# The causal mask of the diagonal scores: a second, accumulating bf16 matmul in place of a select on GpSimd

## What is computed

```python
q = (x @ wq_w.T + wq_b).reshape(b, t, H, HD)        # b=2, t=2048, H=32, HD=32
k1, v1 = x @ wk_w.T + wk_b, x @ wv_w.T + wv_b       # one head for keys and values
scores = jnp.einsum('bqhd,bkd->bhqk', q, k1) / jnp.sqrt(jnp.float32(HD))
scores = jnp.where(causal, scores, -jnp.inf)
weights = jax.nn.softmax(scores, axis=-1)
attn = jnp.einsum('bhqk,bkd->bqhd', weights, v1).reshape(b, t, H * HD)
x = _layernorm(x + attn @ wo_w.T + wo_b)
x = _layernorm(x + ffn(x))      # ffn: scaled, clipped x times scaled, clipped weight, scaled back
```

## Time and profile before

| | us |
|---|---|
| three runs, median (lowest to highest) | 2768.05 (2760.64 to 2773.67) |
| profiled execution: span | 2772.0 |
| the run nearest to that span | 2773.67 |
| PE busy | 2549.6 (92%) |
| DVE busy | 1861.1 (67%) |
| ACT busy | 1276.1 (46%) |
| POOL busy | 843.5 (30%) |

### The profile page before, as it was taken

How to read it: one execution, slowest core, us unless ns; L and a number is a source line. 1 busy time by engine, 2 the same in 40 slices (tenths; PEclk the granted TensorE clock), 3 DMA queues, 4 the chain that set the end, 5 groups by cost and what they waited for, 6 DMA issues and landing times.

```text
span 2772.0 us, 45699 instructions
## 1 busy us (share of the span) xinstructions
PE 2549.6 (92%) x15400; PEld 1588.9 (57%) x15400; DVE 1861.1 (67%) x1428; ACT 1276.1 (46%) x1571; POOL 843.5 (30%) x568
## 2 busy tenths in 40 slices
PE   6999994989999999999888999999999998699998
PEld 5888883544555444444455554554444446588887
DVE  6333335557688898989646677898898894444444
ACT  2222222545566766677425556666676671100000
POOL 2321302423222221231323323232212314466663
PEclk9999996889999999999889999999999998799999
DMA  6343334522111120110224112111101013122221
GB/s 231 119 151 129 121 121 128 133 51 65 50 39 39 39 57 20 38 38 27 66 83 121 51 38 66 39 50 38 39 27 38 12 28 144 46 91 91 91 91 61
DMA packets 78806, 201.42 MB, mean 73 GB/s; under 512 B 8704, under 2 KB 10752, under 8 KB 76544
## 3 DMA queue, kind: packets, MB, share of 16 engines
q1 hardware_dynamic: 51936, 142.11, 18.0%
q10 hardware_dynamic: 26784, 58.21, 5.5%
HBM read 125.83 MB, written 74.45 MB: 72 GB/s over the span
## 4 chain that ended last, share of the span: by engine, by line
PE 77%; issue 6%; DVE 4%; POOL 4%; ACT 4%; DMA 2%; ACTq 1%; SPq 1%; DVEq 0%; POOLq 0%
PE bank L1112 16%; PE bank L1153 15%; PE bank L1100 14%; PE bank L1044 13%; PE bank L1201 13%; ACT prob L678 4%; POOL prob L537 3%; PE bank L1129 3%; PE bank L1121 2%; DMA q_st<-max_d 1%; DVE acc L907 1%; PE bank L1190 1%; PE bank L1028 1%; DMA xt_raw<-x_t 0%; DVE acc L904 0%
## 5 line engine op out<-in xcount | busy, mean ns | idle before, releaser
L678 ACT ACTIVATE prob<-bank 128x1024 f32<-128x1024 f32 (+3 forms) x1280 | 1075.7, 896 | 656.1 <-PE bank L1112 611.7
L907 DVE TENSOR_TENSOR acc<-acc,prob 128x2048 f32<-128x2048 f32 (+3 forms) x512 | 1073.8, 2097 | 171.6 <-POOL prob L537 131.0
L1112 PE MATMUL bank<-q_st,k_st 98*128 98x512 f32 (+3 forms) x2560 | 700.3, 391 | 62.6 <-DMA q_st<-max_d 31.7
L1153 PE MATMUL bank<-prob,v_sb 128*32 128x512 f32 (+3 forms) x5120 | 614.8, 553 | 67.2 <-POOL prob L537 65.0
L1112 PEld LDWEIGHTS bank<-q_st,k_st 98*128 98x128 f32 x2560 | 430.0, 193 | 376.1 <-ACT prob L678 266.3
L537 POOL TENSOR_SCALAR_AFFINE_SELECT prob<-prob 128x512 f32<-128x512 f32 x256 | 282.5, 1106 | 929.4 <-ACT prob L678 928.5
L1153 PEld LDWEIGHTS bank<-prob,v_sb 128*32 128x32 f32 x5120 | 101.8, 109 | 267.9 <-issue 159.3
L1044 PE MATMUL bank<-xt_hi,w_hi 128*128 128x512 f32 x576 | 226.5, 393 | 14.8 <-DVE xt_lo L765 14.8
L1044 PE MATMUL bank<-xt_hi,w_lo 128*128 128x512 f32 x576 | 226.1, 393 | 0.0
L1044 PE MATMUL bank<-xt_lo,w_hi 128*128 128x512 f32 x576 | 225.7, 392 | 0.0
L1201 PE MATMUL bank<-wf_hi,xs_hi 128*128 128x512 f32 x512 | 202.4, 395 | 0.0
(11 more groups left out here) (118 smaller groups left out, 2654.1 us busy)
## 6 DMA issues: line engine op xcount, KB each, us to landing
q_st<-q_hi_d SPq DMA_DIRECT2D x128, 256.0 KB
xt_raw<-x_t SPq DMA_DIRECT2D x16, 1024.0 KB, 6.5
q_hi_d<-part_hi ACTq DMA_DIRECT2D x64, 256.0 KB, 2.1
q_lo_d<-part_lo ACTq DMA_DIRECT2D x64, 256.0 KB, 2.3
q_st<-q_lo_d SPq DMA_DIRECT2D x64, 256.0 KB
x<-x_d SPq DMA_DIRECT2D x32, 512.0 KB, 3.3
out<-y ACTq DMA_DIRECT2D x32, 512.0 KB, 2.6
res<-x SPq DMA_DIRECT2D x24, 512.0 KB, 3.5
```

Source lines behind the costliest of these rows:

```text
L678: nc.scalar.activation(prob[:, t % SLOTS, 2 * p:2 * p + 2, off:NB], bank[:, 2 * p:2 * p + 2, off:NB], ACT.Exp, scale=SCALE).then_inc(p_don ...
L907: nc.vector.tensor_tensor(acc[:, r, :, off:NB], acc[:, r, :, off:NB], new, ALU.add).then_inc(acc_done, 1)
L1112: last = nc.tensor.matmul(bank[:, h, off:NB], k_st[:, t * P:(t + 1) * P], q_st[:, slot, h, off:NB], start=True, stop=True)
L1153: last = nc.tensor.matmul(bank[h * HD:(h + 1) * HD, 4 + r, off:NB], v_sb[:, t], prob[:, t % SLOTS, h, off:NB], start=(t == 0), stop=(t == ...
```

## The change

The select on POOL and its semaphore are gone. On diagonal steps each score matmul is left open (`stop=False`) and followed by a matmul of 128 columns in bf16 that adds `mask_bf` transposed, through `ident_bf`, onto the triangle's columns of the same bank; the exponential of -3e38 is then 0. The value product and DVE's sums wait for `p_done` alone. On POOL `res + bo` follows `att_lo` directly. Since the first score tile of block 0 is diagonal and that of block 1 is not, the last pair of block 0 is written out behind its loop on every engine instead of being its last turn.

```diff
             for j in range(JB):
-                first, last = int(j == 0), int(j == JB - 1)
+                first, last = int(j == 0), int(j in (0, JB - 1))
...
                 if last:
-                    body(j, G // 2 - 1, False, True)
+                    body(j, G // 2 - 1, False, j == JB - 1)
...
                         nc.gpsimd.tensor_tensor(att_lo[:], heads, att_hi[:].bitcast(F32), ALU.subtract).then_inc(att_cut, 1)
-                    for r in range(2):
-                        n, s0 = group(b, j, gp, r), step(b, j, gp, r)
-                        for i in range(QT):
-                            t = QT * j + i
-                            off = first_query(j, t)
-                            wait_apart(pool, p_done, s0 * 2 + (2 * t + 4))
-                            tri = prob[:, t % SLOTS, :, off:off + P]
-                            nc.gpsimd.affine_select(out=tri, in_=tri, compare_op=ALU.is_ge, fill=0.0, base=0,
-                                                    pattern=[[0, HG], [1, P]], channel_multiplier=-1).then_inc(masked, 1)
-                        if j > 0 and r == 0:
-                            pool.wait_ge(res_in, stored_alone(b, j, gp) * 16 + 16)
-                            nc.gpsimd.tensor_tensor(res[:], res[:], bo[:], ALU.add).then_inc(res_ready, 1)
-                    if j > 0:
+                        pool.wait_ge(res_in, stored_alone(b, j, gp) * 16 + 16)
+                        nc.gpsimd.tensor_tensor(res[:], res[:], bo[:], ALU.add).then_inc(res_ready, 1)
                         inverse_deviation(moments[:, 0], ln1, tile * LN + LN)
...
                                 dve.wait_ge(p_done, s0 * 2 + (2 * t + 4))
-                                if t >= QT * j:
-                                    dve.wait_ge(masked, n * QT + (t - QT * j + 1))
...
-                def scores(s0, j, slot, t):
+                def scores(s0, j, slot, t, own):
...
                         for h in (2 * p, 2 * p + 1):
-                            last = nc.tensor.matmul(bank[:, h, off:NB], k_st[:, t * P:(t + 1) * P], q_st[:, slot, h, off:NB], start=True, stop=True)
+                            last = nc.tensor.matmul(bank[:, h, off:NB], k_st[:, t * P:(t + 1) * P], q_st[:, slot, h, off:NB], start=True, stop=not own)
+                            if own:
+                                last = nc.tensor.matmul(bank[:, h, off:off + P], mask_bf[:], ident_bf[:], start=False, stop=True)
                         last.then_inc(s_done, 1)
...
                             if t + 1 < NT:
-                                scores(s0, j, r, t + 1)
+                                scores(s0, j, r, t + 1, t + 1 >= QT * j)
                             elif not (last_pair and r == 1):
                                 pe.wait_ge(q_in, n * 64 + 128)
-                                scores(s0 + NT, 0, 1 - r, 0)
+                                leaves_first_block = r == 1 and isinstance(gp, int) and gp == G // 2 - 1
+                                scores(s0 + NT, 0, 1 - r, 0, j == 0 and not leaves_first_block)
...
                             pe.wait_ge(p_done, s0 * 2 + (2 * t + 4))
-                            if t >= QT * j:
-                                pe.wait_ge(masked, n * QT + (t - QT * j + 1))
```

More of the change, by code:

```diff
@@ L227, in build @@
         p_done = sem("p_done")
-        masked = sem("masked")
         pv_done = sem("pv_done")
@@ L1133, in _ @@
                 pe.wait_ge(q_in, b * (SEQ_GROUPS * 64) + 64)
-                scores(b * SEQ_STEPS, 0, 0, 0)
+                scores(b * SEQ_STEPS, 0, 0, 0, True)
                 def body(j, gp, first, last_pair):
```

## The result

| us | before | after |
|---|---|---|
| median of 20 runs (lowest to highest) | 2763.11 (2757.51 to 2776.08) | 2782.31 (2773.7 to 2784.23) |
| profiled execution: time, span | 2773.67, 2772.0 | 2780.62, 2778.8 |

The ratio after to before, worked out over all the runs, is 1.0053, 95% interval 1.0043 to 1.0063. By it the change costs about 15 us (the two medians alone are 19 apart), where 6 less were forecast; 2782 lies inside the range given (2735 to 2800).

What follows compares the result with a forecast made beforehand. PE was taken as the bound: POOL's delay goes, mask matmuls come, both on PE's queue. Blocks summed -9 - 14.5 + 25 - 7 = -5.5, say 6 us less than 2768: 2762 us, range 2735 to 2800.

Steps and rivals of the forecast that it cites:

- block 0: Attention block 0, 8 pairs: select leaves the path, two masks come in, 1.1 us a pair less; 9 us gained.
- block 1: Attention block 1: six pairs' waits 32 us and a first-pair wait 7.7, less masks 16 x 1.56; 14.5 us gained.
- block 2: Attention block 2: PE has no wait for POOL, so masks are paid in full, 16 x 1.56 = 25 us lost.
- block 3: Attention block 3: waits of 16.1 us in one sequence, 32 in both, less 25 for masks; 7 us gained.
- outside: Span beyond the four blocks' sums: no term forecast there; the pair written out behind block 0's loop costed at nothing.
- The price of a mask: PE, diagonal steps: 0.109 us for three heads, 0.057 for the last; 0.39 a step, 1.56 a group, 100 in all.
- the rival's estimate: Masks behind 128 columns: quick bf16 loads make 256 masks some 0.04 us cheaper each, 10 us, 2752; chance 0.12.
- 6 x (2.8 + 2.5) = 32: Block 1, six pairs: value product 2.78 us late behind the select, plus mean 2.5 us lost to low clock.
- The base of the sum: Whole kernel: profiled execution 2773.67 us, median of runs shown 5.6 below, so -6 was taken from 2768.
- Cheap masks: PE's mask matmuls: no load shows at all, 58 us instead of 100, 2720 us; chance 0.20.
- loads not taken early: PE between bf16 and fp32r: mask's own load shows too, 112 us more, 2870, up to 2946; chance 0.22.
- The moved addition: POOL's res + bo behind att_lo: DVE late in block 3, ACT waits for a slot, 17 us, 2779; chance 0.05.

Runs made afterwards that it cites:

- e1: The kernel after without its 1,024 mask matmuls and with nothing in their place, so the causal mask is left out: 2694.66 us, 0.9746 of before.
- e11: The kernel after with mask and identity in fp32r instead of bf16: 2777.73 us over 12 runs, ratio 1.0037 to before.
- e8: The kernel before, unchanged, profiled a second time: 2769.03 us.
- e3: The kernel before with only the last pair of block 0 written out behind its loop: 2766.63 us over 12 runs, ratio 1.0013.
- e2: The kernel before with the mask matmuls added, POOL still selecting, and block 0's last pair written out: 2825.61 us, ratio 1.0228.
- e4: The kernel after with res + bo back behind the last exponential of r = 0: 2774.87 us, ratio 1.0046 to before.
- e9: The kernel after with masks behind both scores of a half step, and in block 2 the select on POOL: 2729.72 us, ratio 0.9871 to before.
- e10: The kernel after with paired masks only at diagonal steps chosen by PE's earlier waits, all other steps selecting on POOL: 2747.5 us.
- e6: The kernel after with every mask matmul issued twice in a row, constant -1e38: 2831.12 us.

## Why the prediction was wrong

Set against the second profile of before (2769.03 us; its span is 11.5 us below that of after), the forecast's terms compare as follows. "Masks" is after less e1, "select" is this profile of before less e1; differences are taken before rounding.

| us | forecast | measured | masks | select |
|---|---|---|---|---|
| block 0 | -9 | -9.5 | 7.3 | 16.8 |
| block 1 | -14.5 | -3.0 | 24.3 | 27.3 |
| block 2 | +25 | +22.8 | 26.7 | 3.9 |
| block 3 | -7 | -6.6 | 26.0 | 32.6 |
| outside | 0 | +7.8 | 6.5 | -1.2 |
| sum | -6 | +11.5 | 90.9 | 79.3 |

**The price of a mask: right, slightly small.** 1.56 us a group was forecast and 1.67 and 1.63 measured. The next head's key load shows behind the mask, as forecast (0.36 us head to head). The Trainium skill (TensorE: Matmul & The Clock Gate, Weight-path perf modes) has a fast load for 128 weights that are not FP32; the traces of e11 and after agree: a recorded load of 99 ns in bf16 and 197 in fp32r, and 0.03 us a head behind 128 columns (0.04 was the rival's estimate). In the sum it brings nothing (e11): behind the wide columns bf16 is 0.01 us a head slower.

**Blocks 2 and 3: right** within 2.2 us, by the steps given. Without the masks block 3 gained 32.6 us by the end of the select, where the row of waits gave 32; block 2 gained 3.9, where the earlier trace rows gave nothing.

**Block 0: the sum right, its terms not.** The 1.1 us a pair was some 1.3 for the select less 0.2 for the masks, 10 and 2 us in all; measured are 16.8 and 7.3. Both were too small, and that the errors cancel is luck. The clock has a part in the larger gain: from 500 to 570 us it is 0.93 in e8 as in e3, and with the masks it stays up (e2).

**Block 1: the step that failed.** "Six pairs have this wait: 6 x (2.8 + 2.5) = 32". The 2.8 held: 47.9 us with the select and a full clock (e8), 45.0 without it (e1), that is 2.9. The 2.5 for the clock did not: I read it at two waits of one profile and gave it to all six pairs. Already in that profile the last pair of the second sequence took 47.9 us, that is, it lost nothing. In e8 three pairs lose 1.4 to 2.8 us with it and three nothing, by the same wait and the same busy time; in e3 one pair of six loses 1.4, and block 1 took 203.8 and 195.2 us, 10 less than in the profile that I had. So the clock term was 15 us in the forecast and is 5.6 in e8 and 1.4 in e3, and the six pairs gain 23 and 19 us, not 32. The first pair's wait was 7.7 us, but without it and the masks that pair is only 4.4 us shorter (60.17 in e8, 55.72 in e1; 2.8 from e3); in after PE waits 2.5 us for `att_lo` there (3.0 in e1), the wait that was next in line. And a fall of the clock was left there: in the first pair of block 1 of both sequences PE waits 3.2 us for ACT, which holds back an exponential for `att_hi`, before the change as after it; here it is in the second sequence of after, and the clock behind it:

```profile
1523.41 0.69 PE L1098 MATMUL bank<-q_st,k_st 98*128 98x384 f32 x1 [3.21 <-ACT prob L666]
```

```profile
1524.00:1528.00 4.00, 4.00 (x17) 0.50 0.00 0
1528.00:1532.00 4.00, 4.00 (x18) 0.50 0.00 0
```

**The base of the sum: the same mistake once more.** The profile was of an execution at 2773.67 us, and I took its 5.6 us over the median off both kernels alike. But what made it slow was in part what the change takes away, the clock in block 1. In a usual execution there is less of it to gain. The profile of e3 is of such an execution (2765.04 us). Set against it, after differs by -12.8, +2.7, +23.0 and -6.2 us in blocks 0 to 3 and by +8.8 outside, +15.5 together, close to the 15 us of the runs. So beside a usual execution block 1 gains nothing at all, where 14.5 us were forecast.

**Outside attention's blocks** 7.8 us came on top where I had nothing. 5.1 of them lie ahead of the first copy, at the start of attention. 3.9 of the 5.1 are the late rise of the clock (first copy at 501.3 us in after and at 497.4 in e4, which is the same program up to there); the masks of the first group lie in the rest. The late rise is in both profiles of after and, at 499 us, in the first of before, so it isn't the change alone. 1.4 us lie between the sequences (81.9 against 80.5) and 1.3 behind attention. Those between the sequences aren't the masks' either, since e1 has 81.9 there without a mask; their cause is open.

**Rivals.** Cheap masks and loads not taken early are out by e1. The moved addition is out by e4: it did grow to 4.4 us, but with it late the blocks take the same. That masks fill the gaps of the select was in the sum only for block 0. It holds in block 3 too when both are there (e2), but the change has only one of them at a time, so the forecast was right to subtract the masks, taken alone, from the waits, taken alone: 25 and 32 there, 26.0 and 32.6 by e1.

## What to carry to other kernels

Work that moves from a helper engine onto the bounding one should move only where the helper is waited for: taking the mask to PE everywhere cost 23 us in the one block in which nobody waited. Being waited for is not enough: in block 1 the masks cost 24 us and the select 27 (from e8) or 22 (from e3), an even trade. Leaving block 2 alone and issuing the masks in pairs made a loss of 0.5% into a gain of 1.3% (e9). But a wait is not removed step by step where the helper's delay comes from a longer piece of work ahead of it (e10): the next step inherits it. And a stretch of low clock in one profile is a draw: take a second profile of the kernel before, or count the same wait in several places of the first, before giving its cost to each wait, and take the profile of an execution near the median.

## What was not expected of the hardware

- The granted clock fell behind three waits of 2.7 to 2.8 us and not behind three others of 2.7 us in the same execution, with PE busy for the same 5.2 to 5.3 us in 8 and fully busy before (e8). The Trainium skill (TensorE: Matmul & The Clock Gate, Part 1: The HAM clock gate) calls the number of slow matmuls at a kernel's start run-variable; the rows of e8 show the like inside one execution.
- A bf16 matmul of 128 columns behind another with the same type costs 0.056 us with its own load (e6), and 0.10 between fp32r ones (66.1 - 62.8 = 3.3 us for the 32 of a pair).
- The same POOL addition of 1,024 elements takes 4.4 us directly behind `att_lo`, beside DVE's sums of 2,048 elements (after), and 2.7 us behind the last exponential, where DVE has a short sum or none (e4). DVE's sums of 2,048 elements take 2.51 us in the mean in after and 2.41 in e4. Neither difference reached the time.
